# A residual image block on one core: eight x1 chunks held, buffers for counted chunks half as large

## The chip, the core and the metric

The kernel runs on one core of a Trainium2 chip. The metric is the device time of one execution in microseconds (us). Engines by their names in the profile: PE (TensorE, matmuls), DVE (VectorE), ACT (ScalarE), POOL (GpSimd) and SP (SyncE), which issues most of the DMAs here. All arithmetic is in f32.

## The reference

Input x is 8 images of 128 channels and 256 x 256 pixels. Cut to what matters:

```python
# layer 0, the residual around a shifted 1x1 convolution
z  = gn(x)                                  # 32 groups of 4 channels
s  = bilinear_shift(z, theta_s) * w_dw      # per channel, a fraction of a pixel
x1 = x + w_pw @ s
# layer 1, the residual around a block in the wavelet domain
h   = haar_dwt(gn(x1))                      # 512 channels, 128 x 128
h   = gelu(batchnorm(w_c1 @ h + b_c1))      # over all images; y1 = before the norm
o   = dwconv3x3(h) + b;  o = layernorm_chw(o)
h2  = w_pw2 @ gelu(w_pw1 @ o + b) + b + h
g   = gelu(batchnorm(w_c2 @ h2 + b_c2))     # 512 channels
out = x1 + haar_idwt(g)
```

## The kernel before

Three stages follow each other. An image is cut into 32 chunks of 8 rows (`CH` = 2048 values per partition, 1 MB); four chunks (`SLOTS`) are a group, eight groups an image. In the middle stage a tile is 1024 values per partition, 16 tiles an image, 128 in all.

**First stage**, 8 images. Each image is read twice. Once it is counted: DVE's `bn_stats` over three quarters of each chunk (`count_x`, L1229), ACT's sum and sum of squares over the last quarter (`sum_x`, L673 and L676); the semaphores `x_counted` and `x_summed` tell of it. Image 0 is counted alone at the start. Image b + 1 is counted while image b is shifted: in step T = (g, s) of image b the chunk (g + 1, s) of image b + 1. Before, image 0's first group counted group 0 of image 1 and then, after its steps, group 1 by itself.

A step of image b works on one chunk of the ring (`load_ring`, L357):
- DVE (`shift_rows`): three `scalar_tensor_tensor` of a whole chunk, up (L1333), down (L1349) and left (L1359), with the counting between them; in some steps (`three_in_v`) a fourth, right (L1365). Ahead of L1333 it waits for its chunk and, for s = 0, 1, 2, for the next one of the ring (`slot_in[near]`). At s = 3 the second instruction needs the next group's first row, copied by POOL (`copy_bottom`).
- PE (`conv`): for each half two matmuls with `w_right` on u (L936) and two with `w_center` on v (L941), added to x, which ACT put into PSUM (L605).
- ACT: `make_y1` of an earlier chunk (L688), `sum_x`, `square_y1` (L709), `take_x1` of both halves (L642), the store of x1 to `out` (L649), `put_x` (L605), and x1's squares (L659), in this order for each step.
- PE (`c1`, L963) makes y1 of image b - 1 from x1, which SP reads back from `out` (`load_x1`, L375). `HELD` = 6 chunks of an image stay in SBUF (`x1_buf`, `x1_more`) and are not read back.

SP issues in the order written: for each step `load_ring`, `load_x1`, `load_x_ahead`, each behind its own waits. `load_x_ahead` (L346) reads the chunk to be counted into `ahead[s]`, four buffers of a chunk:

```python
wait_alone(sp, nth(b * NCH + g * SLOTS + s, SLOTS), x_counted, x_summed)
sp.dma_start(ahead[s], x[b, :, bass.ds((g * SLOTS + s) * CH, CH)]).then_inc(ahead_in[s], 16)
```

`nth(t, k)` is the value of a counter when chunk t - k is done, so the load waits for both counts of the chunk four back. At the seams of images DVE, PE and ACT work out the norms (`x_moments`, `group_variance`, `x_scales`, `x1_moments`, `c1_weights`). After image 7 its y1 is made, 32 chunks by PE.

**Middle stage**, 128 tiles. `bn1_ready` follows the statistics of y1. Then step s makes h of tile s (ACT, L804), puts one tap into PSUM (L833), adds taps on PE (`add_pe_taps`, L1087; three taps for the first `HEAD` = 18 tiles, part of one later), on POOL (`pool_tap`, L550, sums L564, L571) and on DVE (`add_tap`, L1458; `finish_o`, L1469), squares o (`square_o`, L850), and, `OLD_LAG` = `RING` - 1 = 19 steps later, runs tile q = s - 19 through `first_conv` (L1039), gelu (L813), `second_conv` (L1046), `make_h2` (L1445), and turns it for the Gram matrix (L1058, L822, L1070). At `norm_step` (s = 18 + 16b) the layer norm of image b is worked out: `o_moments`, `group_variance`, `o_weights`, and one step later `o_bias`. Each tile's o lives in a ring of 20. Then the covariance of h2 gives the second batch norm's scales.

**Output stage**, 256 chunks: `second_bands` on PE (L1142), four gelus on ACT (L891), four additions on DVE, a halving on ACT (L898), and POOL's DMA that adds the chunk to `out` (L578).

## Time and profile before

| | us |
|---|---|
| median of 3 runs | 5347.55 (5343.45 to 5351.78) |
| the profiled execution | 5349.64, span 5348.0 |
| PE, DVE, ACT, POOL busy | 4636.7, 4607.9, 4341.1, 1152.0 |
| read from and written to HBM | 877.35 MB, 662.70 MB |

Busy times are of one execution, seen by the hardware profiler; matmul ends are modelled. A matmul of f32 stands as two records. In the windows of the trace each engine has its busy time and, in brackets, its instructions, then the clock that PE was granted (1.00 is the higher of its levels), the mean busy share of the 16 DMA engines and what they moved. In the timeline brackets hold the engine's idle time ahead of an instruction and who ended it.

### The profile page before, as it was taken

How to read it: one execution, taken by the hardware profiler on the slowest of the kernel's cores; microseconds unless marked ns; L12 is line 12 of the kernel's file. 1: busy time of each engine (PE TensorE's matmuls, PEld its weight loads, DVE VectorE, ACT ScalarE, POOL GpSimd, SP SyncE). 2: the span in 40 equal slices, each digit the busy share in tenths (PEclk: the TensorE clock that was granted, in tenths of full speed). 3: DMA queues.
4: the chain of work that ended last, by engine and by line, in shares of the span. 5: the costliest groups of instructions: out<-in, count | busy, mean ns of one | idle time of the engine just before them, and what ended most of it. 6: DMA issues, size and time to landing. Idle time of an engine off the chain costs nothing. (4 is left out here: it accounts for less than half of the span.)

```text
span 5348.0 us, 54815 instructions
## 1 busy us (share of the span) xinstructions
PE 4636.7 (87%) x12574; PEld 2144.3 (40%) x12574; DVE 4607.9 (86%) x4207; ACT 4341.1 (81%) x6467; POOL 1152.0 (22%) x855
## 2 busy tenths in 40 slices
PE   2789999999999999999998999999987777777775
PEld 1233334344343443444443666666642222222222
DVE  7999899898998989999907999999568888888887
ACT  5788888888888888888846888888578888888887
POOL 0000000000000000000005888888301111111111
PEclk7999999999999999999999999999999999999998
DMA  8999999999999999998972333333159999999999
GB/s 337 346 351 362 426 404 414 425 383 425 394 414 425 381 425 400 416 405 332 381 283 95 134 134 135 136 136 135 51 113 225 236 236 236 236 235 236 235 236 224
DMA packets 248866, 1542.05 MB, mean 288 GB/s; under 512 B 29424, under 2 KB 29808, under 8 KB 91504
## 3 DMA queue, kind: packets, MB, share of 16 engines
q1 hardware_dynamic: 156528, 936.14, 44.9%
q0 software_dynamic: 36864, 268.45, 24.2%
q10 hardware_dynamic: 55296, 335.57, 15.0%
q8 instruction: 53, 0.87, 0.1%
q14 instruction: 125, 1.02, 0.1%
HBM read 877.35 MB, written 662.70 MB: 288 GB/s over the span
## 5 line engine op out<-in xcount | busy, mean ns | idle before, releaser
L1142 PE MATMUL ps<-arena,c2T 128*128 128x512 f32 x2048 | 1024.3, 651 | 366.8 <-ACT arena L891 364.5
L963 PE MATMUL ps<-arena 128*128 128x512 f32 x2048 | 980.8, 623 | 40.2 <-DMA arena<-out_x 23.3
L941 PE MATMUL ps<-arena 128*128 128x512 f32 x2048 | 966.0, 598 | 45.1 <-DVE arena L1365 22.4
L936 PE MATMUL ps<-arena 128*128 128x512 f32 x1536 | 740.7, 605 | 79.7 <-DVE arena L1349 35.2
L1142 PEld LDWEIGHTS ps<-arena,c2T 128*128 128x128 f32 x2048 | 401.4, 205 | 989.0 <-ACT arena L891 559.7
L891 ACT ACTIVATE arena<-ps,small 128x512 f32<-128x512 f32 x1024 | 713.7, 778 | 98.6 <-DVE arena L1574 90.1
L1333 DVE SCALAR_TENSOR_TENSOR arena<-arena,shift 128x2048 f32<-128x2048 f32 x256 | 601.8, 2351 | 162.0 <-DMA arena<-in_x 100.9
L1458 DVE SCALAR_TENSOR_TENSOR ps<-arena,taps,ps 128x256 f32<-128x256 f32 (+1 forms) x604 | 655.8, 1133 | 19.6 <-PE ps L1087 19.0
L605 ACT ACTIVATE ps<-arena 128x1024 f32<-128x1024 f32 x512 | 526.4, 1028 | 159.8 <-ACT arena L642 146.9
L521 POOL TENSOR_SCALAR arena<-arena 128x256 f32<-128x256 f32 x112 | 103.9, 936 | 2518.8 <-DMA arena<-in_x 2387.3
L642 ACT ACTIVATE arena<-ps,small 128x1024 f32<-128x1024 f32 x512 | 565.0, 1104 | 91.1 <-PE ps L941 89.3
L963 PEld LDWEIGHTS ps<-arena 128*128 128x128 f32 x2048 | 388.8, 192 | 577.7 <-issue 568.8
L941 PEld LDWEIGHTS ps<-arena 128*128 128x128 f32 x2048 | 386.6, 191 | 566.2 <-issue 469.2
L1359 DVE SCALAR_TENSOR_TENSOR arena<-arena,shift 128x2048 f32<-128x2048 f32 x256 | 599.1, 2340 | 3.5
L1349 DVE SCALAR_TENSOR_TENSOR arena<-arena,shift 128x2048 f32<-128x2048 f32 x256 | 598.6, 2338 | 1.9
L898 ACT ACTIVATE arena<-arena 128x2048 f32<-128x2048 f32 x256 | 490.4, 1916 | 113.5 <-DVE arena L1582 110.7
L1229 DVE BATCH_NORM_STATS2 arena<-arena 128x512 f32 (+1 forms) x768 | 497.2, 681 | 20.9 <-DMA arena<-in_x 20.9
L578 POOL DMA_DIRECT2D out_x<-arena x256 | 218.1, 852 | 1320.2 <-ACT arena L898 1287.2
L1581 DVE TENSOR_TENSOR arena<-arena 128x1024 f32<-128x1024 f32 x256 | 314.3, 1228 | 209.5 <-DMA out_x<-arena 208.5
L659 ACT ACTIVATE arena<-arena 128x2048 bf16<-128x2048 f32 x256 | 484.8, 1894 | 0.5 <-ACT arena L642 0.5
L936 PEld LDWEIGHTS ps<-arena 128*128 128x128 f32 x1536 | 287.1, 191 | 476.6 <-issue 350.0
L564 POOL TENSOR_TENSOR arena<-arena 128x1024 f32<-128x1024 f32 x128 | 302.9, 2367 | 99.6 <-ACT arena L840 54.5
(169 smaller groups left out, 5907.7 us busy)
## 6 DMA issues: line engine op xcount, KB each, us to landing
arena<-in_x SPq DMA_DIRECT2D x508, 1024.0 KB, 14.4
out_x<-arena ACTq DMA_DIRECT2D x256, 1024.0 KB, 9.0
out_x<-arena POOLq DMA_DIRECT2D x256, 1024.0 KB, 17.0
arena<-out_x SPq DMA_DIRECT2D x208, 1024.0 KB, 16.7
y_dram<-arena ACTq DMA_DIRECT2D x128, 512.0 KB, 8.5
arena<-y_dram SPq DMA_DIRECT2D x128, 512.0 KB, 3.6
h_dram<-arena SPq DMA_DIRECT2D x112, 512.0 KB, 2.7
arena<-h_dram SPq DMA_DIRECT2D x112, 512.0 KB, 10.2
```

The costliest lines, as they stand in the source:

```text
L605: nc.scalar.activation(banks(half), ring[:, bass.ds(1 + s * ROWS + half * 4, 4), :] .rearrange("p r c -> p (r c)"), ACT.Copy).then_inc(x_i ...
L642: nc.scalar.activation(x1_made(s, place)[:, half * (CH // 2):(half + 1) * (CH // 2)], banks(half), ACT.Identity, bias=bias0, accum_out=tot ...
L891: last = nc.scalar.activation(g_buf[k][:, q, :], ps[:, 4 * k + q, :], ACT.Gelu, bias=z_bias[:, q:q + 1], scale=z_scale[:, q:q + 1])
L936: mm(ps[:, r, :], w_right[:, :], u_buf[k][:, 2 * r:2 * r + 2, 2:W + 2], start=False, stop=False, skip_group_check=True)
L941: last = mm(ps[:, r, :], w_center[:, :], v_buf[k][:, r * BANK:(r + 1) * BANK], start=False, stop=True, skip_group_check=True)
L963: last = mm(ps[:, 4 + s % 2, :], w_c1b[:, q, :], cells[:, q // 2, q % 2, :, :], start=(q == 0), stop=(q == 3))
L1142: last = mm(ps[:, 4 * k + q, :], c2T[:, q, :], h2[:, k * HC:(k + 1) * HC], start=True, stop=True)
L1229: last = nc.vector.bn_stats(stats_x[:, bass.ds(i * (6 * DVE_PIECES) + 6 * r, 6)], chunk[:, r * BANK:(r + 1) * BANK])
L1333: stt(out=u, in0=ring[:, s * ROWS:(s + 1) * ROWS, :], scalar=up, in1=slot(s), op0=ALU.mult, op1=ALU.add).then_inc(u_up, 1)
L1349: stt(out=u, in0=ring[:, s * ROWS + 2:(s + 1) * ROWS + 2, :], scalar=down, in1=u, op0=ALU.mult, op1=ALU.add).then_inc(u_done, 1)
L1359: left_added = stt(out=v, in0=u_buf[k][:, :, 0:W], scalar=left, in1=u, op0=ALU.mult, op1=ALU.add)
L1458: stt(out=acc, in0=h_tile(t, dy, dx, first), scalar=tap_weight(dy, dx), in1=acc, op0=ALU.mult, op1=ALU.add).then_inc(dw_acc, 1)
```

## The change

In the first stage:
- `HELD` is 8: `x1_more` has four chunks; `load_x1` reads back 24 chunks of an image.
- `ahead` is four half chunks. A chunk to be counted comes in two transfers of 512 KB, and its load waits for both counts of the chunk two back.
- `counted_piece` replaces the choice of buffer. The first eight chunks of image 1 are loaded whole into `x1_buf` and `x1_more` and counted in pairs in the four steps of image 0's first group. Image 0's own counting uses `x1_more` instead of `ahead`.
- In image 0 the step s = 1 of each group leaves its left shift to PE (`left_on_pe`, `w_left`): four matmuls more, one DVE instruction fewer.

Between the stages: seven banks are primed at the start and the last one before image 7's y1; the edges of `h_rows` and the ones in `hT_buf` are set, and the first two y1 tiles loaded, while that y1 is made.

In the middle stage: `RING` is 21 and `HEAD` 19. `pool_b` and `o_squares` are gone: ACT's product goes straight into `pool_sum`, and squares (from tile 15 on all in the late place, at the end of ACT's step s = t + 2) are written there too. Weights and bias of `pw1` have two copies each. On PE the norm's products stand after the convolutions, on ACT its square root after the put, on DVE its moments after the first tap. The covariance is worked out from the Gram matrix without the two products of the mean.

```diff
-HELD = 6
-ARENA = 50960
+HELD = 8
+ARENA = 51300
-HEAD = 18
+HEAD = 19
-RING = 20
+RING = 21
...
-        ahead = [cut(CH) for _ in range(SLOTS)]
+        ahead = [cut(CH // 2) for _ in range(SLOTS)]
...
+        def squared_late(t):
+            return t < NT - 1
...
+        def counted_piece(b, g, s, r):
+
+            if isinstance(b, int) and (b == 0 or b == 1 and isinstance(g, int) and g < 2):
+                chunk, arrived, count = first_chunk(g, s) if b == 0 else \
+                    (x1_more[s], more_in[s], 8 * NG + 16) if g else (x1_buf[s], second_in[s], 16)
+                return chunk[:, r * BANK:(r + 1) * BANK], arrived, count
+            k = s % 2 * 2 + r // 2
+            return ahead[k][:, r % 2 * BANK:(r % 2 + 1) * BANK], ahead_in[k], \
+                b * (8 * NCH) + g * (8 * SLOTS) + (s // 2 * 16 + 16 - 8 * (NCH + 2 * SLOTS))
+
+        def left_on_pe(b, s):
+            return isinstance(b, int) and b == 0 and s == 1
...
-                wait_alone(sp, nth(b * NCH + g * SLOTS + s, SLOTS), x_counted, x_summed)
-                sp.dma_start(ahead[s], x[b, :, bass.ds((g * SLOTS + s) * CH, CH)]).then_inc(ahead_in[s], 16)
+                if not (isinstance(b, int) and b == 1 and isinstance(g, int) and g == 2 and s < 2):
+                    wait_alone(sp, nth(b * NCH + g * SLOTS + s, 2), x_counted, x_summed)
+                for half in range(2):
+                    k = s % 2 * 2 + half
+                    sp.dma_start(ahead[k], x[b, :, bass.ds((g * SLOTS + s) * CH + half * (CH // 2), CH // 2)]
+                                 ).then_inc(ahead_in[k], 16)
...
+            sp.wait_ge(setup_done, 1)
             for s in range(SLOTS):
-                load_x_ahead(1, 0, s)
+                sp.dma_start(x1_buf[s], x[1, :, s * CH:(s + 1) * CH]).then_inc(second_in[s], 16)
+            for s in range(SLOTS):
+
+                wait_alone(sp, nth(NCH - SLOTS + s), x_counted, x_summed)
+                sp.dma_start(x1_more[s], x[1, :, (SLOTS + s) * CH:(SLOTS + s + 1) * CH]).then_inc(more_in[s], 16)
...
-                nc.scalar.activation(o_squares, o_ring[t % RING], ACT.Square,
+                nc.scalar.activation(a_buf if squared_late(t) else pool_sum[t % 2], o_ring[t % RING], ACT.Square,
...
-                if 0 <= s - 3 < TILES and (s - 3) % NT != NT - 1:
+                if s >= 3 and squared_late(s - 3):
                     square_o(s - 3)
...
+                if pairs:
+                    count_x(1, *pairs[0])
+                elif ahead_of and not late:
                     count_x(*ahead_of, s, range(0, 2))
```

## Rows read from the trace of the kernel before

**Rows 1.** Windows of the trace: image 0, image 3, a group of image 7, later stages.
```profile
99.10:401.20 302.10, 237.81 (x505) 93.82 (x506) 288.90 (x232) 241.39 (x389) 15.64 (x14) 0.94 0.88 330
1065.90:1399.70 333.80, 317.76 (x713) 134.18 (x712) 304.48 (x246) 281.85 (x513) 10.62 (x14) 0.98 0.99 408
2498.20:2533.20 35.00, 35.00 (x82) 15.11 (x81) 32.98 (x14) 30.11 (x48) 2.52 (x2) 1.00 0.99 392
2930.00:3806.00 876.00, 847.18 (x4008) 546.84 (x4009) 853.96 (x1021) 741.45 (x920) 763.09 (x439) 1.00 0.37 131
3806.00:3911.00 105.00, 102.33 (x522) 67.35 (x521) 22.06 (x27) 35.92 (x50) 0.00 (x0) 1.00 0.01 6
3925.00:5348.00 1423.00, 1023.79 (x2048) 400.86 (x2047) 1185.97 (x1024) 1194.79 (x1280) 218.09 (x256) 0.93 1.02 230
```
The columns are: stretch, its length, then PE, PEld, DVE, ACT and POOL busy, PE's clock, DMA share, GB/s.

**Rows 2.** The same windows: the first and a later group of image 0.
```profile
99.10:153.70 54.60, 31.56 (x64) 12.53 (x64) 42.02 (x39) 35.10 (x62) 0.81 (x2) 0.81 0.71 264
222.50:256.80 34.30, 29.59 (x64) 11.47 (x64) 34.30 (x26) 30.05 (x49) 2.43 (x2) 1.00 0.98 370
```

**Rows 3.** The same windows: groups of image 3.
```profile
1106.00:1147.20 41.20, 40.81 (x90) 17.68 (x91) 36.89 (x27) 34.12 (x62) 1.33 (x2) 0.96 0.85 319
1147.20:1185.70 38.50, 38.50 (x89) 16.62 (x88) 36.77 (x27) 34.13 (x64) 2.66 (x2) 1.00 1.01 426
1185.70:1225.50 39.80, 39.09 (x89) 16.46 (x88) 36.92 (x26) 34.23 (x65) 0.81 (x2) 1.00 1.01 425
1225.50:1267.70 42.20, 40.52 (x92) 16.95 (x91) 37.02 (x27) 36.65 (x67) 0.95 (x2) 1.00 1.01 425
...
1310.90:1354.90 44.00, 41.28 (x93) 16.74 (x93) 37.23 (x26) 39.01 (x70) 1.44 (x2) 1.00 1.01 426
1354.90:1399.70 44.80, 38.86 (x88) 16.53 (x87) 43.08 (x50) 36.70 (x70) 0.00 (x0) 0.96 1.01 422
```

**Rows 4.** DMA queues from 1268 to 1355: packets, MB, share of 16 engines.
```profile
q1 hardware_dynamic: 3543, 25.87, 70.7%
q10 hardware_dynamic: 1875, 11.15, 30.6%
```

**Rows 5.** Timeline of DVE in image 0: start us, us, line, what.
```profile
205.21 2.34 DVE L1333 SCALAR_TENSOR_TENSOR arena<-arena,shift 128x2048 f32<-128x2048 f32 x1
...
208.67 2.33 DVE L1349 SCALAR_TENSOR_TENSOR arena<-arena,shift 128x2048 f32<-128x2048 f32 x1
...
222.48 2.34 DVE L1333 SCALAR_TENSOR_TENSOR arena<-arena,shift 128x2048 f32<-128x2048 f32 x1
```

**Rows 6.** Timeline of ACT in the same stretch.
```profile
210.79 1.11 ACT L642 ACTIVATE arena<-ps,small 128x1024 f32<-128x1024 f32 x1 [0.33 <-PE ps L941]
...
216.63 0.19 ACT L676 ACTIVATION_READ_ACCUMULATOR arena<-arena 128x1 f32 x1
```

**Rows 7.** Ring loads (L357) issued from 190 to 400, from issue to landing.
```profile
DMA to landing us min/median/max: 5.0/8.9/14.6
```

**Rows 8.** Timeline of PE in the same stretch.
```profile
207.16 1.88 PE L936 MATMUL ps<-arena 128*128 128x512 f32 x4
208.88 1.88 PE L941 MATMUL ps<-arena 128*128 128x512 f32 x4
```

**Rows 9.** Timeline at the start of the middle stage.
```profile
2819.74 7.40 PE L969 MATMUL ps<-c2T,ident 128*128 128x512 f32 x12 [6.43 <-DVE arena L1437]
...
2828.41 13.79 PE L1087 MATMUL ps<-arena,tap_diag 128*128 128x384 f32 x33 [1.27 <-ACT ps L833]
```

**Rows 10.** Timeline at the norms of the middle stage, images 0 and 2.
```profile
2932.20 2.98 PE L1039 MATMUL ps<-arena 128*128 128x512 f32 x4 [2.67 <-DVE arena L1469]
...
3172.75 0.19 DVE L1485 TENSOR_REDUCE small<-sums_o 128x2 f32<-128x32 f32 x1 [0.73 <-ACT arena L850]
```

**Rows 11.** Timeline of the covariance, first and last of DVE.
```profile
3915.56 0.15 DVE L1542 TENSOR_SCALAR small<-gram 128x1 f32<-128x1 f32 x1
...
3924.30 0.17 DVE L1563 TENSOR_TENSOR small<-small,bn 128x4 f32<-128x4 f32 x1
```

More of the change, by code:

```diff
@@ L419, in load_first_image @@
                     load_ring(0, 1, s)
-                    load_x_ahead(1, 1, s)
-                for s in range(SLOTS):
                     load_x_ahead(1, 2, s)
@@ L732, in shift_group @@
                             act.wait_ge(mom_ready, b * 2 + 2)
-                        sum_x(*ahead_of, s)
+                        if first and isinstance(b, int) and b == 0:
+                            for pair in first_pairs(s):
+                                sum_x(1, *pair)
+                        else:
+                            sum_x(*ahead_of, s)
                     if chunk:
@@ L745, in image @@
             def image(b, before, tail, following, beyond):
-                first_image = isinstance(b, int) and b == 0
-                shift_group(b, 0, before, tail, (b + 1, 0 if first_image else 1) if following else None, "first")
-                if first_image:
-                    for s in range(SLOTS):
-                        sum_x(1, 1, s)
+                shift_group(b, 0, before, tail, (b + 1, 1) if following else None, "first")
                 shift_group(b, 1, before, tail, (b + 1, 2) if following else None, "second")
@@ L998, in image @@
                 shift_group(b, 1, before, tail, "second")
-                with pe.Fori(2, NG - 1) as g:
+                shift_group(b, 2, before, tail, "")
+                with pe.Fori(3, NG - 1) as g:
                     shift_group(b, g, before, tail, "")
@@ L1003, in _ @@
             pe.wait_ge(setup_done, 1)
-            for bank in range(6):
+            for bank in range(7):
                 last = prime(bank)
@@ L1335, in shift_rows @@
                 late = last and s == 0
+                pairs = first_pairs(s) if first and isinstance(b, int) and b == 0 else None
                 if first and s == 1:
@@ L1343, in shift_rows @@
                     group_variance(nx, gmom_x, ps_small_x)
-                if ahead_of and not late:
+                if pairs:
+                    count_x(1, *pairs[0])
+                elif ahead_of and not late:
                     count_x(*ahead_of, s, range(0, 2))
@@ L1380, in image @@
             def image(b, before, tail, following, beyond):
-                first_image = isinstance(b, int) and b == 0
                 for s in range(SLOTS):
-                    shift_rows(b, 0, s, before, tail, (b + 1, 0 if first_image else 1) if following else None, "first")
-                if first_image:
-                    for s in range(SLOTS):
-                        count_x(1, 1, s)
+                    shift_rows(b, 0, s, before, tail, (b + 1, 1) if following else None, "first")
                 with dve.Fori(1, NG - 1) as g:
@@ L1418, in _ @@
             c1_weights(B - 1, 2 * B)
+            dve.wait_ge(c1_done, nth((B - 1) * NCH + HELD - 1))
+            dve.wait_ge(x1_stored[SLOTS - 1], 16 * (B * NG) + 16)
+            for edge in (0, HW + 1):
+                nc.vector.memset(h_rows[:, :, edge], 0.0)
+            for k in range(2):
+                last = nc.vector.memset(hT_buf[k][:, :, P], 1.0)
+            last.then_inc(edges_made, 1)
             dve.wait_ge(y1_ready, nth(B * NCH, 1))
@@ L1513, in _ @@
                 gram_end = q >= NT + 1 and (q - 1) % NT == 0
-                if b is not None:
-                    o_moments(b)
-                for n, (t, i) in enumerate(tap_order(s)):
+                ops = tap_order(s)
+                for n, (t, i) in enumerate(ops):
                     if i == len(dve_taps(t)):
@@ L1520, in _ @@
                         add_tap(t, i)
-                    if n == 0 and after is not None:
+                    if n == 0 and b is not None:
+                        o_moments(b)
+                    if n == 2 and after is not None:
                         o_bias(after)
```

183 lines of the change are left out of this document (95 added, 88 removed).

## Prediction, made before the change was run

> **What bounds the kernel now.** I read the busy times by stage first, then those of the groups of four chunks inside one image, then single steps in the timeline, and last the times from issue to landing.
>
> By stages [rows 1]: the profiled execution has a span of 5348.0 us (5349.6 with what lies around it, against a median of 5347.55, so the span can stand for the median). Image 0 of the first stage takes 302.1 us, images 1 to 6 about 333.8 each (the row is image 3), a group of four chunks in image 7 35.0, the middle stage 876 in its steady part, the output stage 1423. The output stage moves 230 GB/s with its DMA share at 1.02, the same read-modify-write of `out` before and after; the change does not touch it, so it keeps its time.
>
> Image 0 [rows 2]: a steady group takes 34.3 us with DVE busy for all of it; its first group takes 54.6 and DVE is busy for 42.0 of them, so 12.6 are stalls. Image 3 [rows 3]: the group at 1147 takes 38.5 with PE busy all the time. It holds 44 matmuls (28 of `conv`, 16 of `c1`), 0.875 us each. The three groups from 1225.5 to 1354.9 take 42.2 to 44.0 at 425 to 426 GB/s, with both PE and DVE waiting at times: transfers bound them. A group with x1 loads moves 17 chunks' worth (4 ring, 4 counted, 4 x1 in, 4 x1 out, 1 of y1), 17 x 1.049 MB / 426 GB/s = 41.9 us. The group at 1106 moves 319 GB/s only, and the last one (44.8) has DVE busy for 43.1: x's moments. So images 1 to 6 are bound by PE and DVE in their first groups, by transfers in the middle, by DVE at the end.
>
> **Eight chunks held.** Two loads of 1 MB fewer in each of seven images. At 426 GB/s that is 2 x 2.46 = 4.9 us of transfer each. But the two are asked for at the seam of the groups at 1106 and 1147 [rows 3], where the rate is 319 at first and PE full afterwards. There a transfer hides behind PE; the groups from 1225 on keep their 17. Gain: 0 if nothing carries over, 4.9 if all of it does; I take none beyond the group times worked out below. Image 7 counts nothing, runs 35.0 us a group with PE full [rows 1], and gains nothing.
>
> **Counted chunks in halves.** Twice as many transfers for the same bytes. In the saturated stretch 1268 to 1355 [rows 4] q1, all 8 KB packets, moved 25.87 MB in 70.7% of 16 x 87 us, 26.3 bytes per ns; q10, where some 600 of 1230 data packets are of 4 KB, moved 11.15 MB in 30.6%, 26.2. So a half costs no more than its half of the bytes; at most 3% of 2.46 us a chunk, 2.4 us an image, and I take 1.8. The Trainium skill (DMA: Bandwidth & Descriptors, Bandwidth) asks for batches of at least 1 MiB to reach three quarters of the peak and gives 6.15 us for a lone one, which speaks against halves. By its fixed cost the 64 halves of an image would cost far more than 1.8 us; the rate at 4 KB packets here disagrees, as long as transfers queue up.
>
> **The wait on two chunks back.** This is what I think decides. `load_x_ahead` had to wait for the counts of chunk T-4, which was always long past. Now it waits for both counts of chunk T-2, DVE's and ACT's, and SP issues in order: behind that waiting instruction stand ring load T+1 and the x1 load. DVE's step T begins only when ring chunk T+1 is in its slot (for s = 0, 1, 2; s = 3 needs it somewhat later, through the bottom row that POOL copies). So DVE's step T now hangs on ACT's second sum of step T-2.
>
> How late is that sum? In image 0, chunk 10 starts on DVE at 205.21 [rows 5] and ACT's second sum for it ends at 216.63 + 0.19 = 216.82 [rows 6], 11.6 us later; chunk 12 starts at 222.48 [rows 5], 5.7 us after that sum. In these 5.7 us the new order has to fit: 0.25 to wake SP, two issues for the halves (0.45 each), then the ring load. A lone 1 MB read lands after 5.0 us at the least, 8.9 in the median of image 0 [rows 7]. Lower bound 1.15 + 5.0 = 6.2, upper 1.15 + 8.9 = 10.0. With the halves ahead of it in an otherwise empty queue the ring chunk ends one chunk time behind them: 0.25 + 5.0 + 2.5 + 0.2 = 8.0, which I take. All of it is over 5.7, so the step starts late, and the loop has to be closed to see by how much.
>
> Image 0, from s = 0 to the next s = 0: DVE step of s = 0, 8.6 (two steps from 205.21 to 222.48) [rows 5]. Step s = 1 is the one with its left shift on PE now: u is ready 208.67 + 2.33 - 205.21 = 5.8 after its start, then 12 matmuls, 6 pairs at 1.72 (207.16 to 208.88) [rows 8] = 10.3. Then ACT: from the taking of half 1 at 210.79 to the sum's end at 216.82, 6.05 [rows 6]. Then 8.0. Sum 8.6 + 5.8 + 10.3 + 6.05 + 8.0 = 38.8 us per group against 34.3. Without the loop it would be 34.3 - 2.25 (the third instruction of s = 1 gone from DVE) = 32.1, held up to 33 by ACT (8.2 a step). So six groups cost 4.5 more each, +27. The last group has the same loop, with x's moments on top: +3. With the bounds 6.2 and 10.0 the group is 37.0 to 40.8.
>
> The first group gains. Both groups of image 1 that are counted early are now in buffers of their own, loaded without waiting, counted in pairs inside the steps. Work: 42.0 busy less 2.25; I take 42 for 54.6, -12.6. Image 0: -12.6 + 27 + 3 = +17 (bounds +6 and +29; if the loop does not bind -23: -12.6, 7 x -1.4, +0.5 for two small DVE operations in the scales).
>
> Images 1 to 6: the same loop with PE's `c1` in it: 8.6 + 5.2 (three pairs after v) + 10.5 (`c1` and `conv`, 12 matmuls of 0.875) + 6.05 + 0.85 (make_y1's instruction) + 8.0 = 39.2. The PE-bound group was 38.5: +0.7 to 1. In the groups bound by transfers 39.2 leaves 3 us for a queue, so these stay at their bytes: 41.9 + 0.3 for halves + 0.3 = 42.5. But the group at 1186 took 39.8 [rows 3] by drawing on what was read ahead, four counted chunks deep; with two in stock it goes to 42.5, +2.7. The three groups after it took 129.4 (1225.5 to 1354.9), since that stock was refilled while DVE waited; now 3 x 42.5, -1.9. The last group's late counts now hold up the ring as well: +1.2. The first: +1. Sum 0.8 + 2.7 - 1.9 + 1.2 + 1 = 3.8, and 0.7 because DVE can no longer run two steps ahead of ACT and even out long and short steps: +4.5 an image, six images +27. Bounds: -2.5 (all bytes saved count, no wait grows) and +12 (loop and queue add up).
>
> **From the first stage to the middle.** Before, bn1_ready releases the y1 loads and six primes: PE's primes start at 2819.74 and last 7.4, the first taps start at 2828.41 [rows 9]. Primes and loads now come earlier; the scales, one h tile (1.24) and one put (1.12) remain, so taps can start near 2821.8. The primes ran slowly after PE's idle time, 7.4 us for 12 records (0.62 each, against 0.43 in [rows 8]); the first taps will take that over, some 1.6 us: -6.6 + 1.6 = -5 (bounds 0 and -7).
>
> **Middle.** Tiles: 4008 PE records in 876 us, 36 a tile (4 `pw1`, 4 `pw2`, 8 turns, 16 of the gram, 4 taps), is 7.87 us a tile; the tail has 522 records in 105 us, 32 a tile, 6.4 [rows 1]. One tile moves to the head, where PE puts six tap halves, 6 x 0.86 = 5.2: -2.7. One more step runs in the tail: +6.4. The norm of an image is made one step further ahead of the first `pw1` that needs it: PE waited 2.67 for that at 2932 [rows 10], and the last norm has the same place: -3 and -3. o_moments no longer waits 0.73 for the last square [rows 10]: seven times, -5. Squares now come last in ACT's step and share a buffer with the products; no row prices that, DVE, PE and POOL are each busy for 87 to 97% of the 876 us, so the bounds are -0.05 and +0.1 on 108 tiles; I take +2. Sum -5 (bounds -14 and +8).
>
> **Covariance.** From 3915.56 to 3924.30 [rows 11] there are five passes between PE and DVE; two go: -2.
>
> **Sum.** 17 + 27 - 5 - 5 - 2 = +32: 5347.55 + 32 = 5379.5 us.
>
> **Rivals.**
> (a) The loop does not bind, because ACT catches up when DVE waits and the reads land quicker than 6.2. For it: ACT's share in image 3 is 282 of 334 us [rows 1]. Against it: ACT's 6.05 us contain hardly a gap [rows 6]. The group's other parts come to 30.8 us, so a steady group under 33 needs the ring chunk within 2.2 us of the sum, or a mistake in my reading of who waits. Image 0 -23, images 1 to 6 near 0, the rest -12: -35, 5312. This is the other side.
> (b) The loop binds in image 0, but the images after it get all the relief of the bytes: 17 - 15 - 12 = -10, 5337.
> (c) Loop and queue add in the groups bound by transfers, whose q1 and q10 are full already [rows 4]: +12 each for six images, image 0 at +29: 72 + 29 - 12 = +89, 5437.
> (d) The middle's dead heat goes wrong by 0.1 to 0.2 a step: +15 on top of the forecast, 5395; inside the range.
> (e) Halves cost by the transfer, not by the byte. Of a lone read's 5.0 us 2.5 are not data [rows 7]; if half of that lands on the ring chunk, 8.0 becomes 9.3: +1.3 in 6 groups of image 0 and in the 2 groups of each of six images that transfers do not bind, +23, 5403. The Trainium skill's rule named above would have it so.
>
> **Chances.** Forecast 0.51, (d) 0.10, (e) 0.05, (a) 0.14, (b) 0.07, (c) 0.13. The forecast's own bounds are 5345 to 5408. Eight in ten: 5315 to 5430, which leaves out most of (a) and the far part of (c). About 0.2%, 10.7 us, is what a measurement of this kernel can tell from no change: faster than 5337: 0.20; within: 0.09 (the low edge of the forecast and part of (b)); slower than 5358: 0.71.
>
> **What would show it.** In image 0 groups near 39 us, with DVE's shift instruction (first of a step) waiting on a read, and SP waiting on ACT's second sum ahead of each half; the first group near 42. In image 3 the group at +80 us no faster than 39, and flat ones near 42.5 after it instead of a rise from 39.8 to 44. GB/s of the steady groups of image 0 near 325 instead of 370. First taps within 9 us of the last y1 statistics. If DVE's first instruction in image 0 waits for nothing, the loop is wrong and (a) holds. If images 1 to 6 come out below 333 us each, the price of the smaller stock is wrong.

## The result, and where it went

The changed kernel takes 5633.76 us (median of 4 runs, 5623.46 to 5636.93), the kernel before 5345.97 on the same chip: 5.3% slower, ratio 1.0531 (95% interval 1.0519 to 1.0544). The forecast was 5379.5, the range ended at 5430. The sign and the mechanism came as forecast, the size did not. By stages, from the two profiled executions (spans 5633.7 and 5348.0, difference 285.7):

| part | before | after | difference | forecast |
|---|---|---|---|---|
| image 0 | 302.1 | 351.3 | +49.2 | +17 |
| images 1 to 6 | 1988.7 | 2215.1 | +226.4 | +27 |
| image 7 | 272.9 | 271.3 | -1.6 | 0 |
| last step of the first stage to the first finished tile | 177.9 | 172.8 | -5.1 | -5 |
| first finished tile to the last h2 tile | 1070.4 | 1090.0 | +19.6 | -5 |
| from there to the end | 1436.8 | 1433.9 | -2.9 | -2 |

(An image runs from DVE's first shift instruction in it to that of the next, image 7 to that of its last step. What is missing to 285.7 is rounding and 0.2 us ahead of image 0.)

First the stretches in windows of the changed kernel: image 0, one of its steady groups, two groups of image 3 (its second and its fourth), image 3, the middle. The columns are those of [rows 1].

```profile
99.30:450.60 351.30, 272.83 (x577) 113.83 (x578) 272.27 (x225) 243.72 (x392) 13.60 (x14) 0.91 0.75 278
...
272.90:315.30 42.40, 34.06 (x72) 14.28 (x72) 32.34 (x23) 29.57 (x48) 2.92 (x2) 0.92 0.78 289
...
1243.80:1289.80 46.00, 40.47 (x91) 16.41 (x89) 36.90 (x26) 36.30 (x67) 3.00 (x2) 1.00 0.84 297
...
1335.10:1381.00 45.90, 40.66 (x92) 16.65 (x90) 36.99 (x25) 37.02 (x67) 2.77 (x2) 1.00 1.01 404
...
1192.90:1565.30 372.40, 327.85 (x708) 136.61 (x708) 305.22 (x245) 284.93 (x514) 16.27 (x14) 0.95 0.94 360
...
3109.80:4199.80 1090.00, 1042.91 (x4731) 659.49 (x4729) 969.53 (x1149) 845.48 (x1057) 815.62 (x469) 0.99 0.31 113
```

The work is that of before (image 3: DVE 305 us busy against 304, ACT 285 against 282, [rows 1]), so what was added is waiting. In image 0 nothing is full: in the steady group shown PE is busy for 34.1 of 42.4 us, DVE for 32.3, and the DMA share is 0.78. In image 3 that holds for the groups up to 1335, with shares of 0.84 to 0.87. From there on the DMA share is 0.97 to 1.01 again, at 376 to 404 GB/s where the groups of before moved 425 [rows 3]. Where nothing is full, look for a circle of waits. Who waits for whom stands in the waits of SP, here of the changed kernel (who waited, for what, us in total, times, longest):

```profile
SPq L361 <- ACT arena L706: 1867.8, 209, 17.6
```

and the same pair before the change:

```profile
SPq L335 <- ACT arena L676: 306.5, 131, 8.0
```

L706 is ACT's second sum (L676 before), L361 the helper in which SP waits (L335 before). SP now stands 1868 us in front of that sum. What is queued behind it shows in the page of the profile, in the costliest lines and in the DMA issues (last number: us to landing):

```profile
L1000 PE MATMUL ps<-arena 128*128 128x512 f32 x2048 | 1036.0, 652 | 167.1 <-DMA arena<-out_x 139.4
...
L1364 DVE SCALAR_TENSOR_TENSOR arena<-arena,shift 128x2048 f32<-128x2048 f32 x256 | 602.4, 2353 | 415.0 <-DMA arena<-in_x 334.7
...
arena<-in_x SPq DMA_DIRECT2D x292, 1024.0 KB, 8.4
...
arena<-in_x SPq DMA_DIRECT2D x432, 512.0 KB, 5.3
arena<-out_x SPq DMA_DIRECT2D x192, 1024.0 KB, 11.8
```

and in the page of before:

```profile
L1333 DVE SCALAR_TENSOR_TENSOR arena<-arena,shift 128x2048 f32<-128x2048 f32 x256 | 601.8, 2351 | 162.0 <-DMA arena<-in_x 100.9
...
arena<-in_x SPq DMA_DIRECT2D x508, 1024.0 KB, 14.4
```

L1364 is DVE's first instruction of a step (L1333 before): it idles 415 us before its 256 executions, 335 of them, before 108 of the executions, put down to a read of `x`; before the change it was 162 and 101 us. `c1` (L1000) waits 139 us for x1 loads, which stand behind the same instruction of SP (23 before). The reads themselves land sooner than before (8.4 us against 14.4 for 1 MB of `x`): they are late because they are asked for late.

One turn of the circle, in image 0:

```profile
218.61 0.19 ACT L706 ACTIVATION_READ_ACCUMULATOR arena<-arena 128x1 f32 x1
...
219.03 0.85 SPq L375 DMA_DIRECT2D arena<-in_x  x2
...
220.31 0.33 SPq L387 DMA_DIRECT2D arena<-in_x  x1
...
229.29 2.35 DVE L1364 SCALAR_TENSOR_TENSOR arena<-arena,shift 128x2048 f32<-128x2048 f32 x1 [7.86 <-issue]
```

The sum of step 10 ends at 218.80. SP issues the two halves of a counted chunk at once, then ring chunk 13, which lands 8.79 us after its issue, at 229.10. DVE's step 12 starts 0.19 us later, 10.49 us after the sum. (The view puts DVE's 7.86 us down to "issue"; it is the landing that shows what DVE waited for.) The forecast had 8.0, with an upper bound of 10.0. I call this time R, and D the time from DVE's first instruction of a step to the end of ACT's second sum in it. R is counted from a sum to the start of the step two later, so two steps take D + R and a group takes twice that by definition, whether a read held the step or not; it only tells where the time lies. Over steps 8 to 25 of an image (mean of the four means by s): image 0 of the changed kernel D 12.15, R 10.15, twice their sum 44.6 (mean of its second to seventh group 44.2); image 3 D 12.9, R 10.1, 46.0 (45.6). In image 0 before D was 11.9 and the time from the sum to the start of the step two later 5.25, which was no wait: the ring chunk had landed 2.6 us ahead in the median.

Not every step is held by its read. The four steps after the one above:

```profile
239.66 2.35 DVE L1364 SCALAR_TENSOR_TENSOR arena<-arena,shift 128x2048 f32<-128x2048 f32 x1 [1.72 <-DMA arena<-in_x]
...
245.98 2.33 DVE L1364 SCALAR_TENSOR_TENSOR arena<-arena,shift 128x2048 f32<-128x2048 f32 x1
...
256.21 2.35 DVE L1364 SCALAR_TENSOR_TENSOR arena<-arena,shift 128x2048 f32<-128x2048 f32 x1 [1.59 <-PE ps L979]
...
272.88 2.35 DVE L1364 SCALAR_TENSOR_TENSOR arena<-arena,shift 128x2048 f32<-128x2048 f32 x1 [8.00 <-PE ps L979]
```

In each of the groups from step 12 to step 27, s = 0 and s = 1 start 0.2 us after the landing of the last ring chunk that they need, the one after their own (so does the one at 272.88, whatever the view names), s = 2 follows s = 1 without a wait, and s = 3 waits 1.59 us for PE, which has its `u` buffer. In image 3, from step 12 on, s = 0, 1 and 2 all start 0.2 to 0.4 us after such a landing.

The landing of ring loads (L387) issued from 190 to 400, after the change:

```profile
DMA to landing us min/median/max: 6.2/8.2/11.7
```

8.2 against 8.9 in [rows 7], although from 181 to 330 only 290 GB/s were moved. I had taken 5.0 for a lone read and 2.5 for what is ahead of it. The 5.0 of [rows 7] is the shortest landing there and not that of a lone read: in the kernel before it was issued at 378.1, and 1.75 MB were moved before it landed.

### The profile page after: what moved, and what is told of

It is laid out like the page before. It is cut to its first block and busy times, and to the rows that moved or that the text cites. A ratio compares the mean times of both kernels' runs of the same rounds, so it can differ in the third digit from the quotient of the medians.

```text
span 5633.7 us, 55407 instructions
## 1 busy us (share of the span) xinstructions
PE 4756.7 (84%) x12634; PEld 2189.5 (39%) x12634; DVE 4604.4 (82%) x4199; ACT 4348.9 (77%) x6469; POOL 1169.2 (21%) x853
## 3 DMA queue, kind: packets, MB, share of 16 engines
q1 hardware_dynamic: 185328, 919.37, 44.2%
## 5 line engine op out<-in xcount | busy, mean ns | idle before, releaser
L1000 PE MATMUL ps<-arena 128*128 128x512 f32 x2048 | 1036.0, 652 | 167.1 <-DMA arena<-out_x 139.4
L979 PE MATMUL ps<-arena 128*128 128x512 f32 x2048 | 974.2, 604 | 43.7 <-DVE arena L1402 30.3
L1364 DVE SCALAR_TENSOR_TENSOR arena<-arena,shift 128x2048 f32<-128x2048 f32 x256 | 602.4, 2353 | 415.0 <-DMA arena<-in_x 334.7
L969 PE MATMUL ps<-arena 128*128 128x512 f32 x1536 | 753.2, 614 | 112.6 <-DVE arena L1383 64.2
L924 ACT ACTIVATE arena<-ps,small 128x512 f32<-128x512 f32 x1024 | 713.0, 778 | 98.8 <-DVE arena L1615 90.0
L552 POOL TENSOR_SCALAR arena<-arena 128x256 f32<-128x256 f32 x112 | 125.4, 1125 | 2771.5 <-DMA arena<-in_x 2763.5
L1000 PEld LDWEIGHTS ps<-arena 128*128 128x128 f32 x2048 | 402.8, 201 | 755.5 <-issue 739.5
L1497 DVE SCALAR_TENSOR_TENSOR ps<-arena,taps,ps 128x1024 f32<-128x1024 f32 (+1 forms) x602 | 654.9, 1131 | 27.2 <-PE ps L1126 25.1
L979 PEld LDWEIGHTS ps<-arena 128*128 128x128 f32 x2048 | 391.3, 193 | 574.3 <-issue 503.1
L969 PEld LDWEIGHTS ps<-arena 128*128 128x128 f32 x1536 | 293.4, 194 | 505.6 <-issue 440.2
L718 ACT ACTIVATE arena<-ps,small 128x512 f32<-128x512 f32 x256 | 172.5, 674 | 206.2 <-PE ps L1000 185.7
```

The lines of the kernel that those rows point to most:

```text
L924: last = nc.scalar.activation(g_buf[k][:, q, :], ps[:, 4 * k + q, :], ACT.Gelu, bias=z_bias[:, q:q + 1], scale=z_scale[:, q:q + 1])
L969: mm(ps[:, r, :], w_right[:, :], u_buf[k][:, 2 * r:2 * r + 2, 2:W + 2], start=False, stop=False, skip_group_check=True)
L979: last = mm(ps[:, r, :], w_center[:, :], rows_, start=False, stop=True, skip_group_check=True)
L1000: last = mm(ps[:, 4 + s % 2, :], w_c1b[:, q, :], cells[:, q // 2, q % 2, :, :], start=(q == 0), stop=(q == 3))
L1364: stt(out=u, in0=ring[:, s * ROWS:(s + 1) * ROWS, :], scalar=up, in1=slot(s), op0=ALU.mult, op1=ALU.add).then_inc(u_up, 1)
L1497: stt(out=acc, in0=h_tile(t, dy, dx, first), scalar=tap_weight(dy, dx), in1=acc, op0=ALU.mult, op1=ALU.add).then_inc(dw_acc, 1)
```

## Experiments

All times are medians; ratios are against the kernel before on the same chip.

**1. The wait alone.** Kernel before:

```diff
-  wait_alone(sp, nth(..., SLOTS), x_counted, x_summed)
+  wait_alone(sp, nth(..., 2), x_counted, x_summed)   # from image 0's second group on
```

> The kernel before, with one number changed: from image 0's second group on, a counted chunk's load waits for the counts of the chunk two back instead of four back (whole buffers, six x1 chunks held, one transfer each). Theory W, that this wait alone makes the loss: from ACT's second sum to DVE's next first instruction the changed kernel shows 10.3 to 12.7 us, and this kernel has the same path, so image 0 goes from 302 to about 360, images 1 to 6 from 333 to 370 to 380 each, in all 5600 to 5680. Rival H, that the halves or the eight held chunks make it: image times as before, 5350 to 5400.

5589.17 us, 1.0448 (1.0426 to 1.0469): +240, close under the expected band. Image 0 346.6, a steady group 41.9, images 1 to 6 together +187. The wait alone makes most of the loss; whole buffers and six held chunks don't protect from it. The windows of this kernel (image 0, a group of it, image 3), DVE's wait, and DVE's first instruction in the four steps of that group:

```profile
99.10:445.70 346.60, 252.30 (x506) 100.25 (x507) 290.08 (x232) 243.09 (x391) 16.20 (x14) 0.88 0.77 284
276.60:318.50 41.90, 31.39 (x66) 12.16 (x64) 34.55 (x25) 30.61 (x49) 2.93 (x2) 0.96 0.81 301
1179.20:1541.10 361.90, 321.32 (x712) 133.09 (x712) 304.88 (x245) 286.24 (x516) 12.67 (x14) 0.99 0.96 377
```
```profile
DVE arena L1334 <- DMA arena<-in_x: 259.4, 99, 7.4
```
```profile
276.59 2.35 DVE L1334 SCALAR_TENSOR_TENSOR arena<-arena,shift 128x2048 f32<-128x2048 f32 x1 [5.46 <-issue]
...
285.16 2.35 DVE L1334 SCALAR_TENSOR_TENSOR arena<-arena,shift 128x2048 f32<-128x2048 f32 x1
...
294.23 2.35 DVE L1334 SCALAR_TENSOR_TENSOR arena<-arena,shift 128x2048 f32<-128x2048 f32 x1 [0.42 <-DMA arena<-in_x]
...
302.80 2.34 DVE L1334 SCALAR_TENSOR_TENSOR arena<-arena,shift 128x2048 f32<-128x2048 f32 x1
```

Here, in image 0, the read holds s = 0 (which starts 0.19 us after its landing in every group), and each other step starts 8.6 to 9.1 us after the one before it, which is about DVE's own time.

**2. The halves alone.** Kernel before, two DMAs of 512 KB into each whole buffer, the wait four back:

```diff
-  sp.dma_start(ahead[s], x[..CH]).then_inc(ahead_in[s], 16)
+  for half in range(2):
+      sp.dma_start(ahead[s][:, half..], x[..CH // 2]).then_inc(ahead_in[s], 16)
```

> The kernel before, with each counted chunk brought by two transfers of 512 KB into the same whole buffer, the wait still four chunks back. Theory W: the transfers queue up and a half costs its bytes, so within 0.3% of before, 5345 to 5365. Rival H, a fixed cost for each of the 224 added transfers of about 1.3 us that lands on the ring chunk: 5420 or more; if halves were the whole cause, 5600.

5365.23 us, 1.0029 (1.0018 to 1.0039): +15.5 for 224 more transfers, 0.07 us each. Image 0 is unchanged (301.4), images 1 to 6 take 3.3 more each. The forecast had 1.8, at most 2.4, an image. By the rule of the Trainium skill (DMA: Bandwidth & Descriptors, Bandwidth) that asks for batches of 1 MiB I had weighed a far higher price; this measurement speaks against it as long as transfers queue up. (The page's table is of DMAs issued from GpSimd; these are issued by SP.)

**3. The changed kernel, with the ring load ahead of the wait.**

```diff
   load_ring(b, g, s); load_x1(b - 1, g - 1, s)
-  load_x_ahead(b + 1, g + 1, s)
+  load_x_ahead(<the counted chunk of the step before>)
```

> The changed kernel, with SP's order turned: each counted chunk's pair of loads is issued one step later, behind the next ring chunk and the next x1 load, so that the wait for counts two back holds up only itself and what comes a step later. Theory Q, that the ring chunk behind the waiting instruction is what DVE waits for: the shift instruction no longer waits; the counted chunk itself is then next, needed 2.35 us after the step's start, and the loop loses about 3.5 us in two steps: groups of image 0 at 37 to 39 instead of 44, images 1 to 6 some 15 to 25 us shorter each, in all 5450 to 5540. Rival S, that two chunks of stock are too few in whatever order: the counted chunk lands as late as the ring chunk did, under 30 us gained, 5600 to 5640.

5403.24 us, 1.01 (1.008 to 1.012): 230 us of the 286 are gone, with the same buffers, halves and wait. Even better than the expected band. DVE's waits in the first stage:

```profile
DVE arena L1278 <- DMA arena<-in_x: 192.5, 123, 3.8
...
DVE arena L1381 <- DMA arena<-in_x: 12.7, 12, 2.2
```

The shift instruction (L1381) hardly waits for its chunk any more (12.7 us in all); `bn_stats` (L1278) waits for the counted one, as foreseen. What I had too high was its landing: a half lands 5.8 us after its issue in image 0 and is needed 2.35 us after the step's start, so the time from the sum to the step two later is 3.6 us in the mean, not 10.15; groups take 35.0 to 36.7.

**4. The rest of the change.** Changed kernel with six held, whole counted buffers, the wait four back:

```diff
-HELD = 8
+HELD = 6
-        ahead = [cut(CH // 2) for _ in range(SLOTS)]
+        ahead = [cut(CH) for _ in range(SLOTS)]
```

(and `load_x_ahead` and its counts as before).

> The changed kernel with six x1 chunks held and whole buffers for counts, one transfer each, four back; the 21-tile ring, the order of the middle and the new first image are kept. Theory W: the whole loss of the first stage was the halves' wait. Image 0 near 279 (302 less 12.6 in its first group, less 1.4 in each other), images 1 to 6 at 331 to 334, the gap to the middle -5, the middle +20 as in the changed kernel's profile, the covariance -3: 5330 to 5345. Rival: the first image or the order loses as well: over 5380.

5351.93 us, 1.0004 (0.9994 to 1.0014): no difference from before. Stage by stage: images 1 to 6 as before (+0.9 in all), image 0 -8.2 instead of -23, transition -5.1, middle +19.7, rest -2.8. So all of the loss of images 1 to 6 comes from what this kernel undoes, the wait, the halves or the eight held chunks. The two odd ones, image 0 and the middle, needed runs of their own.

**5. Left shift back on DVE, ring of 20.**

```diff
-            return isinstance(b, int) and b == 0 and s == 1     # left_on_pe
+            return False
-RING = 21
-HEAD = 19
+RING = 20
+HEAD = 18
```

> The six-held kernel with whole buffers, and two parts of the change undone that lie in different stages: the left shift of image 0's s = 1 is DVE's again, and the ring has 20 tiles (18 in the head). Theory L: in image 0 of the six-held kernel DVE waits 3.2 us for PE once in a group, because PE has the left shift's matmuls to do in one piece (steps 8.57, 7.02, 11.81, 8.57); with it gone from PE all steps are 8.57, groups 34.3 instead of 36.0, image 0 near 285 instead of 294. Rival: PE's added matmuls are free and something else of the new first image costs 1.7 a group: no change, 294. For the middle: a tile less costs 7.4 less in the tail and some 2 more in the head; the head's alternation of 5.15 and 6.01 and the seams' 44.8 stay, so from the first finished tile to the last h2 tile 1083 to 1086 against 1090, 1070 before. In all 5334 to 5342.

5354.26 us, 1.0005 (0.9995 to 1.0015). First stage: groups of 34.3 again, image 0 289.1 (expected 285) against 293.9. The reason stands in DVE's timeline of kernel 4, a step after the one whose left shift PE does:

```profile
303.20 2.34 DVE L1390 SCALAR_TENSOR_TENSOR arena<-arena,shift 128x2048 f32<-128x2048 f32 x1
308.70 2.35 DVE L1358 SCALAR_TENSOR_TENSOR arena<-arena,shift 128x2048 f32<-128x2048 f32 x1 [3.16 <-PE ps L973]
```

DVE starts s = 2 earlier, and then waits 3.16 us at s = 3 until PE, which has four matmuls more in that stretch, gives the `u` buffer back: steps 8.57, 7.02, 11.82, 8.57, 36.0 instead of 34.3. The middle took 1097.6, where I had expected 1083 to 1086. The tail gave its 5.8 us back, but the sum of the five finish intervals at a norm, 43.4 to 46.2 in the changed kernel, grew to between 45.5 and 47.1. The 21st tile had been hiding part of what the new order costs.

**6. Own buffers for product and squares.** Kernel 4 with the ring of 20 and ACT's product in `pool_b`, the squares in `o_squares`, with the waits of before:

```diff
-                elif t >= 2: act.wait_ge(o_squared, nth(t - 2))
-                nc.scalar.activation(rows(pool_sum[t % 2]), h_tile(...), ...)
+                if t: act.wait_ge(pool_step, pool_done(t - 2) + 2)
+                nc.scalar.activation(rows(pool_b), h_tile(...), ...)
```

> The six-held kernel with a ring of 20 tiles, and with the room so gained ACT's products and squares in buffers of their own as before, so that the product of tile t no longer waits until DVE has finished tile t-2; the order of puts, squares and norms stays the new one, the left shift stays on PE. Theory P: the shared buffer makes the head's alternation and the seams' extra; head steps flat at 5.15, four seam intervals back to about the 35.8 of before in their sum, the middle from first finished tile to last h2 1066 to 1072. Rival O: the new order of ACT and PE at the norms makes it; the head goes flat, the seams stay, 1076 to 1080. In all 5330 to 5345, the first stage unchanged.

5350.47 us, 0.9997 (0.9986 to 1.0007), middle 1091.1. Half of theory P held: the head goes flat, 5.15 a tile instead of 5.15 and 6.01 in turns. The seams stay as in kernel 5, to a tenth. So the shared buffer costs the head (6.7 us) and nothing at the norms. In the changed kernel the head reads so (DVE finishes a tile, ACT's product waits for that, PE's taps wait for ACT's put behind it):

```profile
3142.08 1.22 DVE L1508 SCALAR_TENSOR_TENSOR arena<-ps,arena 128x1024 f32<-128x1024 f32 x1
...
3143.34 1.15 ACT L873 ACTIVATE arena<-arena,taps 128x1024 f32<-128x1024 f32 x1 [1.65 <-DVE arena L1508]
...
3145.43 1.10 ACT L863 ACTIVATE ps<-arena,taps 128x1024 f32<-128x1024 f32 x1
...
3146.58 5.85 PE L1126 MATMUL ps<-arena,tap_diag 128*128 128x512 f32 x13 [0.59 <-ACT ps L863]
```

**7. The whole middle as before.** Kernel 6 with the left shift on DVE and ACT's, PE's and DVE's order at the norms as in the kernel before:

```diff
-            return t < NT - 1            # squared_late
+            return t % NT != NT - 1
```

(and `put_tap` behind the root, `norm_product` ahead of `turn_h2`, `o_moments` ahead of the taps).

> The six-held kernel with the left shift on DVE and the whole middle as before (20 tiles, own buffers, norms and squares at their old places). What is left of the change is the first group of image 0, the earlier y1 loads and primes, and the shorter covariance. If the parts are worth what their stages show one by one: image 0 near 285, first stage's end 2645, then 172.8 to the first finished tile, 1070.4 for the middle, 1433.9 for the rest: 5322 to 5326, ratio 0.995. Rival: a stage gives back what another gains (the clock after a shorter idle stretch, the queue), 5335 or more.

5325.07 us, 0.995 (0.9933 to 0.9966): faster than both kernels, as expected. Image 0 289.1, middle

```profile
2822.90:3895.40 1072.50, 1033.07 (x4723) 651.17 (x4721) 962.91 (x1150) 850.54 (x1054) 820.39 (x471) 0.99 0.33 115
```

1072.5 against 1091.1 of kernel 6, transition 173.0, rest 1432.4. The gains of separate stages add up.

**8. Three back.** Kernel before, `nth(..., 3)` where kernel 1 has 2.

> The kernel before with the counted chunk's load waiting for the counts three back instead of four (two back cost 4.5%). Theory W: what counts is whether the ring chunk behind the wait still lands in time. A step more of slack is 8.6 us on top of the 5.7; the path takes 10.4, under 14.3, so image 0 keeps its 302 and the images after it come within 3 us of before: 5345 to 5370. Rival: the cost grows with the stock taken away, half of it at three back: 5450 to 5490.

5374.32 us, 1.0044 (1.0028 to 1.006): +22.5, just above the expected band, a tenth of kernel 1. Image 0 keeps its 301.8 and its groups of 34.4. The cost isn't in proportion to the stock: in image 0 one step more (8.6 us on top of 5.25) covers the 12.3 us that the held step of kernel 1 needs. Images 1 to 6 lose 4 us each. Ring chunks take 14.6 us to land in image 3, 10.2 in image 0, which is the likely reason; no run tests it.

**9 and 10. Which half of the order.** Kernel 7's middle with ACT's order new (9), or with the places of the norms on PE and DVE new (10). In both the left shift is on DVE, other than the expectation of 9 says of it; that concerns image 0 alone.

```diff
 # 9: ACT                                  # 10: PE and DVE
+ put_tap(s)   (ahead of the root)         + norm_product(...)  (behind second_conv)
+ square_o(s - 2) at the end, all tiles    + o_moments(b)       (behind the first tap)
```

> The six-held kernel with a 20-tile ring and own buffers for products and squares (as the one in which the head went flat and the seams stayed long), but with the norms at their old places on PE and DVE; only ACT's order stays new (squares at the end of its step, the put ahead of the norm's root). Its five finish intervals at a norm were 45.5 to 47.1 us with all of the new order, 43.1 to 44.2 with the old one. Theory N, that the places of the norms on PE and DVE cost it: seams back to 43 to 44, the middle 1071 to 1075. Theory A, that ACT's order costs it: seams stay at 45.5 to 47, the middle 1088 to 1092. The left shift stays on PE.

> The counterpart: the same kernel with ACT's order as before and the new places of the norms on PE and DVE. Theory N: seams stay at 45.5 to 47, the middle 1088 to 1092. Theory A: seams at 43 to 44, the middle 1071 to 1075. If each gives a part, the two kernels share the 18.6 us.

5339.72 us (0.9982, 0.9971 to 0.9994) and 5340.36 us (0.9985, 0.9974 to 0.9996). Middle 1083.0 and 1087.3, between 1072.5 with neither and 1091.1 with both. Neither theory alone: each half costs (10.5 and 14.8), and together less than their sum (18.6). Where the wait goes is seen on POOL at one norm: the product it needs comes behind the norm's root, its table loads and the put, and in the changed kernel behind a square too. Changed kernel, then kernel before:

```profile
3461.86 2.36 POOL L592 TENSOR_TENSOR arena<-arena 128x1024 f32<-128x1024 f32 x1 [6.02 <-ACT arena L873]
```
```profile
3185.47 2.36 POOL L564 TENSOR_TENSOR arena<-arena 128x1024 f32<-128x1024 f32 x1 [3.10 <-ACT arena L840]
```

**11. Changed kernel, left shift on DVE, put behind the root.** The edit of 5 for `left_on_pe`, the put of 7, nothing else.

> The changed kernel (eight held, halves, wait two back, 21 tiles) with image 0's left shift back on DVE, and in the middle ACT's put behind the norm's root as before. The loop as the traces show it: a group is twice D + R, D from DVE's first instruction of a step to the end of ACT's second sum (12.15 us in the mean over s in image 0 of the changed kernel, 11.0 in the kernel that has only the wait), R from there to DVE's step two later (10.15 and 10.0). Theory L, that D is longer because PE has the left shift of s = 1: D back to 11.0, groups 44.2 to 42, image 0 351 to 336 to 340. Rival: the halves make D longer: no change. Images 1 to 6 unchanged in both. Middle: if the put ahead of the root costs the seams their 1.3 each, 1080 to 1083 instead of 1090.

5611.62 us, 1.0491 (1.0461 to 1.0521). Image 0 335.6, D 10.7, R 9.8, groups of 41.3: theory L, in full. The same PE work that costs 1.7 us a group with the wait four back (kernel 4 against 5) costs 2.9 inside the circle. Images 1 to 6, to which neither edit applies, came out 21 us shorter in all; no run explains that, and the changed kernel's own runs lie within 13.5. The put expectation fell: 1097.2, not 1080. At the first norm, in the head, one finish interval went from 8.3 to 15.2 us; the later norms stayed. With the norms at their new places the earlier put is worth 7 us, once.

**12. Kernel 1 with the ring load ahead of the wait.** The edits of 1 and 3 on the kernel before.

> The kernel before with the wait two back and with SP's order turned as in the turned changed kernel (each counted chunk's load one step later, behind the next ring chunk and x1 load); whole buffers, one transfer, six held. Theory Q, that the place of the waiting instruction in SP's queue is nearly the whole price: the 240 us of the wait fall to those of a stock of two. The turned changed kernel is 51 us over the six-held one; halves alone cost 15.5 of them, so the stock of two should cost 30 to 40: 5375 to 5395. Rival E, that the rest lies in holding eight or in halves and wait together: 5350 to 5362.

5411.26 us, 1.0113 (1.0096 to 1.013). The order gives back 178 of 240 us, so theory Q holds, but the stock of two costs 61, not 30 to 40, more than in kernel 3 with its halves. DVE's waits in the first stage:

```profile
DVE arena L1246 <- DMA arena<-in_x: 225.5, 133, 6.5
```

Here `bn_stats` waits for a whole megabyte (6.6 us to landing in image 0, 9.4 in image 3), longest 6.5 us; in kernel 3 for a half, longest 3.8. Images 1 to 6 together are 61 us over before here, 48 in kernel 3. Kernel 3 has halves, but it also holds eight chunks, and no run tells the two apart.

## The prediction, point by point

*What bounds before*: nothing seen speaks against it; kernel 4 leaves images 1 to 6 where they were. That eight held chunks bring a gain was seen in no run; but none holds eight with the wait four back, for which the room isn't there, so their worth stays open.

*The wait two back*: the step that decided, and named as such. SP's waits, the ring load behind them and ACT's second sum as releaser are those of the profile, and so is the path in image 0: from s = 0 to s = 1, through PE's work for s = 1 to ACT's sum of s = 2, and from there to the next s = 0, once a group. What failed is the size of its terms. The same path over steps 8 to 25, in us:

| | s = 0 to s = 1 | s = 1 to the sum of s = 2 | sum to the next s = 0 | group |
|---|---|---|---|---|
| image 0, forecast | 8.6 | 22.15 | 8.0 | 38.8 |
| image 0, changed kernel | 11.3 | 23.4 | 9.95 | 44.6 |
| image 0, kernel 1 | 8.7 | 20.8 | 12.3 | 41.8 |
| image 3, forecast | 8.6 | 22.6 | 8.0 | 39.2 |
| image 3, changed kernel | 10.1 | 24.1 | 11.65 | 45.9 |

1. The last term, the time from ACT's sum to DVE, was mis-sized: 10 to 12.3 us for 8.0. The forecast gave 0.25 to wake SP, 7.5 from there to the ring chunk's landing, 0.2 to DVE; the turn shown above has 0.23, 10.07 and 0.19, of the middle one 1.28 for the issues and 8.79 from issue to landing. My upper bound of 10.0 was the better guess, and the median of [rows 7] was at hand: I departed from it downwards on the ground that the queue would be emptier, and it hardly moved.
2. The first term was put at 8.6, DVE's own time, though the forecast itself says that s = 1 too needs a read released by a sum two steps back. In the changed kernel that read is late as well: s = 1 starts 12.7 us after the sum of the s = 3 before it, and 11.3 after s = 0. In kernel 1 it is in time, and the term is 8.7. (In image 3 the reads hold s = 2 as well, so the rows of image 3 say where the time lies, not which wait closes the turn.)

Then a conclusion fell with them: "39.2 leaves 3 us for a queue, so these stay at their bytes". At 46 the circle is longer than the 42.5 of the bytes, and every group of images 1 to 6 pays. In image 3 the first four groups took 28 us more than before (the first alone 10.7, which no run takes apart), where the forecast had 4.5, and the three that I had called bound by transfers 136.7 instead of 129.4. Of the 226 us of images 1 to 6 kernel 1 alone has 187. Rival (c), +12 an image, had the right sign and a third of the size. It let the queue add to the loop in the three groups bound by transfers; the DMA share of 0.97 to 1.01 there fits that, but no run says how much of the 7 us is queue, and the larger part lies in the groups ahead of them.

Of the signs that the forecast named, the waits of DVE and SP came. The sizes did not: steady groups of image 0 of 44.2 us at 289 GB/s, not near 39 at 325, and 45.3 for the group of image 3 at +80 us.

PE showed something else that I had not looked for. The changed kernel, in image 0:

```profile
193.40 1.88 PE L979 MATMUL ps<-arena 128*128 128x512 f32 x4
199.31 3.78 PE L969 MATMUL ps<-arena 128*128 128x512 f32 x4 [4.03 <-DVE arena L1383]
202.88 2.99 PE L974 MATMUL ps<-arena 128*128 128x512 f32 x4
205.71 1.88 PE L979 MATMUL ps<-arena 128*128 128x512 f32 x4
```
```profile
201.00:205.00 4.00, 4.00 (x6) 1.69 (x5) 2.74 (x2) 0.33 (x2) 0.00 (x0) 0.50 0.93 342
```

After 4.03 us without work four matmuls take 3.78 us instead of 1.88, at a granted clock of 0.50 (1.2 GHz) in the window under them. So a wait slows the matmuls that follow it. Counting spacings of 0.78 to 0.95 us between starts instead of 0.43, such matmuls cost 12.7 us in image 0 and 13.8 in image 3, before 6.8 and 5.0. The Trainium skill (TensorE: Matmul & The Clock Gate, HAM oscillation — how this bites in real kernels) describes such bursts between waits for DMA, which start at the low clock each time; the trace agrees, though PE waits here for DVE, which waits for the read. It explains little of the loss: kernel 1 has 5.5 us of it in image 3 and still takes 362 us, and it has 17.6 us of it in image 0, where its D is only 11.0. D is long in image 0 of the changed kernel because of the left shift on PE: without it D is 10.7 (kernel 11).

*Halves*: forecast 1.8 an image, measured 3.3 (kernel 2), over its bound of 2.4. Rival (e) put the cost on the ring chunk of the circle, 1.3 us a turn; what halves cost inside the circle was not measured by itself.

*First image*: the first group gained as forecast, 39.6 against "42 for 54.6". "34.3 - 2.25, held up to 33 by ACT" failed: with no loop in the way kernel 4 needs up to 36.0. (The terms given for that case, -12.6, 7 x -1.4 and +0.5, add up to -21.9, not -23.) I had charged the moved shift to DVE's account and not to PE's, whose matmuls sit between DVE and its `u` buffer.

*Transition* -5.1 for -5, *rest* -2.9 for -2. The last y1 statistics and the first taps, first and last DVE instruction of the covariance:

```profile
3089.39 0.69 DVE L1466 TENSOR_REDUCE part<-ps 128x2 f32<-128x512 f32 x1 [87.98 <-ACT arena L739]
...
3095.36 15.86 PE L1126 MATMUL ps<-arena,tap_diag 128*128 128x384 f32 x33 [8.33 <-ACT ps L863]
```
```profile
4204.14 0.15 DVE L1585 TENSOR_SCALAR small<-gram 128x1 f32<-128x1 f32 x1
...
4209.48 0.17 DVE L1604 TENSOR_TENSOR small<-small,bn 128x4 f32<-128x4 f32 x1
```

6.0 us to the first taps (within 9, as said), and 5.3 us for the covariance against 8.7 in [rows 11].

*Middle*: -5 forecast, +19.6 measured. The tail's step was right (6.4 forecast, 7.4 measured). The dead heat was named but priced at "+0.1 on 108 tiles"; it is not spread over the tiles, where 7.49 stayed 7.49, but sits in the head: 6.2 us, shown by kernel 6. And the gains at the norms (-3, -3 and 7 times -0.73) were counted from waits that were seen, without asking what comes late next. At the norm shown above it was ACT's product for POOL. The five intervals at a norm went from 43.2 to 44.5 in the mean. That the new order costs this is shown by kernels 7, 9 and 10; which instruction of PE's and DVE's new places does it was not taken apart.

*The sum of the parts*: wait 240, halves 15.5, the rest of the change 2.3 make 257.3 of some 286. The rest by stages, from the profiled executions: image 0 has 49.2, of which the parts alone give 44.5, -0.7 and -8.2; 13.6 are left. The left shift on PE costs 15.7 there inside the circle (kernel 11) and 4.8 outside it (kernel 4 against 5), so 11 of the 13.6 are its. Images 1 to 6 have 226.4, of which the parts alone give 186.6, 19.6 and 0.8; 19 are left and stay open. Kernel 11, whose edits don't touch these images, came out 21 us shorter there, so this is no more than two kernels can differ by without a cause that I know.

## To carry to other kernels

When a wait is put into a queue that issues in order, price the path of everything behind it, not the load that waits; the same wait cost 61 us behind the urgent loads and 240 ahead of them. When steps become held by loads that earlier steps release, follow the path from one held step to the next held one, add all latencies of the turn, and count the engine's own time only for the steps that no read holds; ask for each step whether its own read is in time. One step of slack more was a jump here (22 us instead of 240), no slope. Take landing times from the median of like loads in the trace, also where the queue will be emptier.

## What the runs showed of the hardware

- A 1 MB read of `x` into the ring lands after 8.2 us in the median in image 0 of the changed kernel, where 290 GB/s are moved, and after 8.9 in image 0 of before at 360: a fifth less traffic gained less than a microsecond. In image 3, from step 8 to 25, it takes 15.0 before, at 426 GB/s, but 11.3 in kernel 12 at 421: the rate alone does not set it.
- A half (512 KB) lands 4.7 us after its issue in image 0 of the changed kernel (median), the whole one behind two halves after 8.2. With the wait four back, 224 more transfers cost 0.07 us each.
- After 4.03 us without a matmul the next ones ran at the granted clock of 0.50, up to 205.1, with PE at work from 199.3.
